# Attention and routed experts on one core: one VectorE copy for both banks of transposed probabilities, and batch 0's expert logits in four column groups

## What is computed

```python
x = x + tanh(g_xattn) * attention(layernorm(x), ctx, ctx, mask)   # qh, kh, vh: 16 heads of 64
x = x + tanh(g_ffn) * ffn(layernorm(x))

# ffn
logits = xf @ Wg + bg                       # [1024, 8]
idx = argmax(softmax(logits), axis=-1)
h = gelu(einsum('th,ehi->tei', xf, W1) + b1)
y = einsum('tei,eih->teh', h, W2) + b2
out = take_along_axis(y, idx)
```

## Time and profile before

| | |
|---|---|
| median of 3 runs | 199.1 us (198.98 to 364.73) |
| profiled execution | 200.14 us |
| its span, first to last instruction | 198.3 us |
| PE busy | 185.5 us, 94% |
| DVE, ACT, POOL busy | 123.5, 104.9, 89.5 us (62%, 53%, 45%) |
| attention loop of batch 0, of batch 1 | about 37 to 62 us, 110 to 137 us |
| between them | about 62 to 103 us |
| POOL's last start-up instruction (L594) | 3.70 us, 0.09 long |
| ACT's load of bg_sb (L784) and wg_sb (L785) | issued at 16.01 and 16.48 us |
| share of the chain of waits | PE 69%, DVE 21%, issue 3%, ACT 2% |

### The profile page before, as it was taken

The page is one execution under the profiler, slowest core; times in us unless marked ns, Lnnn a source line. Parts: engine busy times, 40 slices in busy tenths (PEclk is TensorE's granted clock), DMA queues, the critical chain, the costliest instruction groups (busy, mean ns, idle before and its releaser), DMA issues.

```text
span 198.3 us, 4265 instructions
## 1 busy us (share of the span) xinstructions
PE 185.5 (94%) x1412; PEld 136.2 (69%) x1412; DVE 123.5 (62%) x538; ACT 104.9 (53%) x376; POOL 89.5 (45%) x128
## 2 busy tenths in 40 slices
PE   7999999999899999999999899998999999999960
PEld 6994455666665444788895666765788899989940
DVE  3479576899996421154459999997833556355520
ACT  3243438899998112211427899997631263445410
POOL 6000002577778991000003899768810024776650
PEclk9999999999999999999999999999999999999996
DMA  4998008999999990480000101600000002353011
GB/s 134 335 369 284 0 3 265 319 287 315 298 317 266 206 326 20 146 279 1 0 2 3 55 27 54 198 0 0 3 0 2 0 3 76 110 153 109 34 53 31
DMA packets 22323, 25.19 MB, mean 127 GB/s; under 512 B 1987, under 2 KB 20877, under 8 KB 22160
## 3 DMA queue, kind: packets, MB, share of 16 engines
q1 hardware_dynamic: 19536, 21.83, 37.3%
q0 software_dynamic: 1152, 2.12, 3.2%
q10 hardware_dynamic: 1600, 0.84, 1.5%
HBM read 14.14 MB, written 11.68 MB: 130 GB/s over the span
## 4 chain that ended last, share of the span: by engine, by line
PE 69%; DVE 21%; issue 3%; ACT 2%; POOL 1%; POOLq 1%; DVEq 0%
PE s_bank L1729 14%; PE o_bank L1674 14%; DVE probs L1308 12%; PE s_bank L2035 8%; PE o_bank L2046 7%; PE s_bank L1769 5%; DVE oT L1335 4%; PE s_bank L1608 3%; PE s_bank L1639 2%; PE o_bank L1817 2%; PE o_bank L1799 2%; PE t_bank L1700 2%; PE s_bank L1844 2%; ACT probs L832 2%; PE s_bank L2024 1%
## 5 line engine op out<-in xcount | busy, mean ns | idle before, releaser
L649 POOL TENSOR_TENSOR probs<-probs,r_col 128x512 f32<-128x512 f32 x32 | 33.3, 1040 | 73.8 <-DVE r_col L1319 73.7
L832 ACT ACTIVATE probs<-probs,negm_run 128x160 f32<-128x160 f32 x128 | 53.0, 415 | 6.1 <-DVE negm_run L1308 5.9
L1308 DVE CUSTOM_DVE_ANT_0 probs<-s_bank,maskneg 128x160 f32<-128x160 f32 x128 | 33.3, 317 | 3.5 <-PE s_bank L1769 3.2
L1729 PE MATMUL s_bank<-xnT,wq_sb 128*128 128x512 f32 x64 | 29.0, 600 | 0.0
L1674 PE MATMUL o_bank<-wo_sb,oT 128*128 128x256 f32 x128 | 28.7, 380 | 0.0
L1674 PEld LDWEIGHTS o_bank<-wo_sb,oT 128*128 128x128 f32 x128 | 23.9, 190 | 3.5 <-issue 0.5
L832 ACT ACTIVATION_READ_ACCUMULATOR probs<-probs,negm_run 128x1 f32 x128 | 23.9, 187 | 0.0
L1769 PE MATMUL s_bank<-k_sb,q_sb 64*128 64x160 f32 x256 | 21.7, 306 | 0.0
L1729 PEld LDWEIGHTS s_bank<-xnT,wq_sb 128*128 128x128 f32 x64 | 11.7, 190 | 13.1 <-issue 12.8
L628 POOL DMA_INDIRECT out_dram<-oT x16 | 17.0, 1064 | 7.8 <-DVE oT L1256 5.9
L1769 PEld LDWEIGHTS s_bank<-k_sb,q_sb 64*128 64x128 f32 x256 | 18.0, 187 | 2.7 <-DVE negm_run L1308 1.5
(11 more groups left out here) (169 smaller groups left out, 299.6 us busy)
## 6 DMA issues: line engine op xcount, KB each, us to landing
sorted_rows<-empty_row SPq DMA_DIRECT2D x8, 1040.0 KB, 15.6
oT<-in_L_ffn_W_dram SPq DMA_DIRECT2D x1, 2048.0 KB, 18.2
q_sb<-in_L_ffn_W_dram SPq DMA_DIRECT2D x1, 2048.0 KB, 9.4
oT<-sorted_rows SPq DMA_DIRECT2D x1, 1040.0 KB, 5.2
oT<-sorted_rows SPq DMA_DIRECT2D x8, 130.0 KB, 2.3
wq_sb<-in_L_xattn_Wq_dram SPq DMA_DIRECT2D x2, 512.0 KB, 8.1
mask_sb<-in_mask_BxSxS_bk_dram SPq DMA_DIRECT2D x2, 512.0 KB, 8.9
wv_sb<-in_L_xattn_Wv_dram SPq DMA_DIRECT2D x1, 1024.0 KB, 10.8
```

The source lines that it names most:

```text
L649: nc.gpsimd.tensor_tensor(window_wide(u), window_wide(u), r.rearrange("p i h -> p (i h)") .unsqueeze(2).broadcast_to([P, 4, WIDE]), ALU.mu ...
L832: last = nc.scalar.activation(window_part(u, i, h), window_part(u, i, h), ACT.Exp, bias=negm_run[at], scale=-1.0, accum_out=l_run[at])
L1308: nc.vector.tensor_tensor_reduce(window_part(u, i, h), s_bank[u % 2][:, h, i * CK:i * CK + WK], maskneg[:, q, 0:WK], -SCALE, LARGEST, ALU. ...
L1729: last = nc.tensor.matmul(bank[m % 4], wq_sb[:, c, m * P:(m + 1) * P], xnT[:, c, b * N:(b + 1) * N], start=(c == 0), stop=(c == DC - 1))
```

## The change

In the attention loop DVE now copies both banks of `t_bank` in one instruction, and ACT copies the left part instead of a bank. In `values` the two waits change places: the left product (first on PE) waits for ACT, the wide one for DVE.

Batch 0's logits are no longer made tile by tile. `batch_logits` makes them transposed, with `wg_sb` (padded with zeros to 32 columns) as the stationary operand and the tokens moving: tile t's logits land on partitions 32t to 32t+31 of bank 5, a group of 32 columns of the array each. DVE copies the 128x128 block to SBUF (`take_logitT`), PE transposes it back (`batch_logits_back`), and `route_logits(0)` reads it from there. The block stands between the second and the third group of keys and the transpose back behind the third; the transposes of tile 3 move ahead of the second group. `wg_sb` and `bg_sb` are cleared first by two memsets on POOL, for which ACT waits before it starts their loads. Batch 1's logits stay as they were.

```diff
-        wg_sb = sb("wg_sb", [P, DC, E])
-        bg_sb = sb("bg_sb", [P, E])
+        wg_sb = sb("wg_sb", [P, DC, LEFT_E])
+        bg_sb = sb("bg_sb", [P, LEFT_E])
+        logitT = sb("logitT", [P, P])
...
-                sp.wait_ge(empty_ready, 2)
+                sp.wait_ge(empty_ready, 4)
...
+            nc.gpsimd.memset(wg_sb[:], 0.0).then_inc(empty_ready, 1)
+            nc.gpsimd.memset(bg_sb[:], 0.0).then_inc(empty_ready, 1)
...
+            act.wait_ge(empty_ready, 2)
...
-            def job_pT_wide(b, job):
-
-                act.wait_ge(first.ptrans_ready, 2 * (b * JOBS + job) + 1)
+            def job_pT_left(b, job):
+
+                act.wait_ge(first.ptrans_ready, 2 * (b * JOBS + job) + 2)
                 if job >= 1:
                     act.wait_ge(first.o_ready, b * JOBS + job)
-                nc.scalar.copy(wide_of_row_half[:, 1], bank[5].rearrange("p (u n) -> p u n", n=DH)).then_inc(first.pT_act, 1)
+                nc.scalar.copy(left_of_row_half, o_bank[:, :, HALF:HALF + P].rearrange("p r (i n) -> p r i n", i=2))\
+                    .then_inc(first.pT_act, 1)
...
+            def take_logitT():
+
+                dve.wait_ge(logit_ps, 1)
+                nc.vector.tensor_copy(logitT[:], bank[5][:, P:2 * P]).then_inc(logitT_taken, 1)
+
...
-            def job_pT_rest(b, job):
-
-                for part, (dst, src) in enumerate((
-                        (wide_of_row_half[:, 0], bank[4].rearrange("p (u n) -> p u n", n=DH)),
-                        (left_of_row_half, o_bank[:, :, HALF:HALF + P].rearrange("p r (i n) -> p r i n", i=2)))):
-                    dve.wait_ge(first.ptrans_ready, 2 * (b * JOBS + job) + 1 + part)
-                    if job >= 1:
-                        dve.wait_ge(first.o_ready, b * JOBS + job)
-                    nc.vector.tensor_copy(dst, src).then_inc(first.pT_dve, 1)
+            def job_pT_wide(b, job):
+
+                dve.wait_ge(first.ptrans_ready, 2 * (b * JOBS + job) + 1)
+                if job >= 1:
+                    dve.wait_ge(first.o_ready, b * JOBS + job)
+                nc.vector.tensor_copy(wide_of_row_half, t_bank[:].rearrange("p r (u n) -> p r u n", n=DH)).then_inc(first.pT_dve, 1)
...
+            def batch_logits():
+
+                pe.wait_ge(xt2_sb, QT)
+                by_tile = [bank[5][t * LEFT_E:(t + 1) * LEFT_E, P:2 * P] for t in range(QT)]
+                for t in range(QT):
+                    nc.tensor.matmul(by_tile[t], bg_sb[0:1, :], ones[0:1, :], start=True, stop=False)
+                for c in range(DC):
+                    for t in range(QT):
+                        last = nc.tensor.matmul(by_tile[t], wg_sb[:, c, :], xnT[:, c, t * P:(t + 1) * P], start=False,
+                                                stop=(c == DC - 1))
+                last.then_inc(logit_ps, 1)
+
+            def batch_logits_back():
+
+                pe.wait_ge(logitT_taken, 1)
+                nc.tensor.transpose(bank[5][:, 2 * P:3 * P], logitT[:], ident[:]).then_inc(logit_ps, 1)
...
                 def transposes(job):
                     if job >= 1:
 
-                        pe.wait_ge(first.pT_dve, b * PER + 2 * job)
+                        pe.wait_ge(first.pT_dve, b * JOBS + job)
...
                 def values(job):
                     quad = job // 2
-                    pe.wait_ge(first.pT_dve, b * PER + 2 * job + 2)
+                    pe.wait_ge(first.pT_act, b * JOBS + (job + 1))
...
-                    pe.wait_ge(first.pT_act, b * JOBS + (job + 1))
+                    pe.wait_ge(first.pT_dve, b * JOBS + (job + 1))
...
                 if where == "k1":
-                    tile_logits(2)
+                    xn2_transposes(3)
                 elif where == "k2":
-                    xn2_transposes(3)
+                    batch_logits()
                 elif where == "k3":
-                    tile_logits(3)
+                    batch_logits_back()
...
-                        tile_logits(0)
...
-                        tile_logits(1)
```

More of the change, by code:

```diff
@@ L314, in flamingo_kernel @@
         logit_ps = sem("logit_ps")
+        logitT_taken = sem("logitT_taken")
         count_ready = sem("count_ready")
@@ L858, in attend_window @@
                         fill(0)
-                    job_pT_wide(b, job)
+                    job_pT_left(b, job)
                 for k in range(1, 4):
@@ L1155, in route_logits @@
                 shape = [P, tiles, E]
-                logits = bank[5][:, at * E:(at + tiles) * E].rearrange("p (t e) -> p t e", e=E)
-                dve.wait_ge(logit_ps, r + 1)
+                if r == 0:
+                    logits = bank[5][:, 2 * P:3 * P].rearrange("p (t e) -> p t e", e=LEFT_E)[:, :, 0:E]
+                else:
+                    logits = bank[5][:, at * E:(at + tiles) * E].rearrange("p (t e) -> p t e", e=E)
+                dve.wait_ge(logit_ps, r + 2)
                 then(nc.vector.tensor_reduce(R.lmax[:], logits, AX.X, ALU.max))
@@ L1385, in attend_window @@
                         window_sum(b, 2 * job + 2)
-                    job_pT_rest(b, job)
+                    job_pT_wide(b, job)
                     also(job)
@@ L1400, in attend @@
                     nc.vector.tensor_copy(*k_dst(u + 1)).then_inc(S.k_dve, 1)
+                    also(f"k{u}")
                 dve.wait_ge(S.mask_ready, n + 1)
@@ L1442, in route_first_batch @@
             def route_first_batch(where):
-                if where == "k":
+                if where == "k1":
+                    take_logitT()
+                elif where == "k":
                     route_logits(0)
@@ L1696, in tile_logits @@
                         nc.tensor.matmul(bank[5][:, q * E:(q + tiles) * E].rearrange("p (t e) -> p t e", e=E),
-                                         ones[0:1, :], bg_sb[0:1, :].unsqueeze(1).broadcast_to([1, tiles, E]),
+                                         ones[0:1, :], bg_sb[0:1, 0:E].unsqueeze(1).broadcast_to([1, tiles, E]),
                                          start=True, stop=False)
                 for c in range(DC):
-                    last = nc.tensor.matmul(bank[5][:, at], xnT[:, c, tt * P:(tt + 1) * P], wg_sb[:, c, :], start=False,
+                    last = nc.tensor.matmul(bank[5][:, at], xnT[:, c, tt * P:(tt + 1) * P], wg_sb[:, c, 0:E], start=False,
                                             stop=(tt in LAST_ROUTED and c == DC - 1))
@@ L2006, in before_projection @@
                 pe.wait_ge(first.pT_act, (b + 1) * (PER if later_too else M))
-                pe.wait_ge(first.pT_dve, (b + 1) * PER)
+                pe.wait_ge(first.pT_dve, (b + 1) * (PER if later_too else M))
             for m in range(M):
```

5 lines of the change are left out of this document (3 added, 2 removed).

## The result

| | before | after |
|---|---|---|
| median | 199.04 us of 4 runs (198.57 to 364.73) | 200.74 us of 4 runs (199.98 to 200.81) |
| profiled execution, its span | 200.14, 198.3 us | 199.98, 198.2 us |
| PE busy | 185.5 us, 94% | 184.7 us, 93% |
| DVE, ACT, POOL busy | 123.5, 104.9, 89.5 us | 127.1, 101.5, 89.5 us |
| chain of waits: PE, DVE, ACT | 69%, 21%, 2% | 65%, 15%, 10% |

The ratio is 1.0085, with a 95% interval of 1.005 to 1.012: the change makes the kernel 1.7 us slower (the run of 364.73 us stands in the median of the table, but not in the ratio). That is clear of the scatter, and less than 2%.

The account below looks back on a forecast made before the run. The loop was taken as bound by the DVE-PE round trip, 3.87 us a job, not by ACT. Terms 0.66+0.05+0.85+0.44 = 2.00 took the median from 199.1 to 201.1 us, range 198.6 to 202.6.

Parts of the forecast that it names:

- the middle: PE work between the batches: logits passes removed 1.65, added 1.30, transpose back 0.20, wait 0.20; sum +0.05 us.
- batch 0's loop: Batch 0's attention loop: steps of 0.22 us at every second max, +0.66 by the output copy before the q projections.
- batch 1's loop: Batch 1's attention loop: later output copy plus DVE's longer leg where it normalises; max 6 comes 0.85 us late.
- batch 1's job 6: Last full chain of batch 1, through ACT's copy: 0.61 us to the wide values becomes 1.05, +0.44.
- The exchange of releasers: values() in the loop: left values wait for ACT behind eight exps, so the output copy is 0.22 us late.
- The two-bank copy: DVE's pT copy in the loop: holds DVE 1.10 us; free under PE's leg, +0.20 where DVE normalises.
- rival 3: Loop: the copy over two banks runs over its cover, up to 0.17 us a job, giving 203.1 us; chance 0.07.
- Rival 1: Loop: ACT is the bound, so 0.19 us is saved in each of twelve jobs, giving 196.9 us; chance 0.10.
- rival 2: Loop: the late start of the left values is absorbed, giving 199.0 to 199.6 us; chance 0.20.
- The block: Batch 0's logits on PE between the batches: 24 passes at 0.037 us plus a 0.41 drain, 1.30 added.
- The removal: Batch 0's old bias and logits tiles on PE: 1.65 us removed in all, 0.97 of it at most ahead.
- The signs: Traces to confirm the forecast: max gaps of 3.87 and about 4.08 us, idle ACT, batch 1's first max 0.7 later.

Follow-up runs that it names:

- e2: The kernel before with only the copies half: attention loop of after, old logits; body 155.60 us, ratio 1.0082 against before.
- e3: The changed kernel with ACT's left copy behind six of the eight exps instead of all; body 153.79 us, ratio 0.9983 against before.
- e5: The changed kernel with a second, unread 256-element ACT copy ahead of each left copy; body 156.60 us, ratio 1.015 against before.
- e7: The changed kernel with DVE copying only bank 4, bank 5 left out; body 154.31 us, ratio 1.0012 against before.
- e8: The changed kernel with POOL normalising only 2 of 32 left keys in batch 1 from unit 8; body 154.63 us, ratio 1.0023 against before.
- e9: The changed kernel with POOL normalising only 16 of 128 wide keys in batch 1 from unit 8; body 154.65 us, ratio 1.0035 against before.
- e1: The changed kernel with the attention loop of before, so only the logits half; body 152.83 us, ratio 0.9964 against before.
- e4: The kernel before with ACT copying 256 of its 512 elements, the rest left out; body 153.29 us, ratio 0.9978 against before.
- e6: e1 with the block of 24 logits passes made twice; body 153.75 us, ratio 1.016 against before.

## Why the prediction was right, and where its terms were off

The sum was 2.00 and the body grew by 1.64; the median went up 1.7. The sign, the mechanism and the place of the loss were right. That the total came so close is partly luck: the middle was put 0.64 too high and batch 1 0.27 too low, and the two errors offset each other in part. The terms against what the traces show:

| term | forecast | measured |
|---|---|---|
| batch 0's loop | +0.66 | +0.67 (the left small transposes behind it start at 61.38 before and 60.97 after, with a first max 1.08 earlier) |
| logits and the middle | +0.05 | -0.59 |
| batch 1's loop | +0.85 | +1.13 (19.54 from its first max to job 6's before, 20.67 after) |
| batch 1's job 6 | +0.44 | +0.43 (its wide values start 4.52 after its first max before, 4.95 after) |

**The exchange of releasers** was right in batch 0 to 0.01 in sum, and nearly so step by step: the left values start 4.32 after M (46.16 to 50.48) where 4.35 was worked out, the wide ones 0.63 later, the output copy 1.13 after these where PE is what it waits for (55.22 to 56.35). e2 shows the loss in this half alone, e3 that it goes with the copy's place, e5 that it is passed on one for one, six times. One detail differed: in job 4 of batch 0 DVE stood idle 0.15 between its first two maxes (the row at 50.51), and that job's exps and left values were 0.25 later than in the jobs before. The profile names no releaser for this idle time; it stands at the same place in after, e2, e3, e5, e7, e8 and e9 and in none of before, e1, e4 and e6, and what makes it stays open. The late step came one job sooner than forecast (4.06 in place of 3.87), and the output copy ahead of the q projections was 0.65 late all the same.

**The two-bank copy**: 1.10 worked out from two sizes, 1.11 measured (126.67 to 127.78), and e7 shows it free in batch 0. DVE doesn't set the pace in batch 0, and rival 3 is out. **Rival 1** (ACT as the bound) is out by e4, and **rival 2** (the late start is absorbed) by after's own gaps of 4.08 and 4.11.

**The middle** was mis-sized by 0.64, at three steps. The block, "24x0.037+0.41 = 1.30", took 0.92: the loads go at 0.15/8 and 0.38/16 us, 0.019 and 0.024 each, not at the 0.037 of L1830, and for 0.20 behind each of the two groups no weights are loaded, not for 0.41 once. That is 0.38. The removal, 0.97 ahead of the first keys, was 1.14: the stretch of the bias and tile 0's logits and transposes shrank from 1.15 (91.05 to 92.20) to 0.22, and the one from the last context transpose to the keys from 1.25 to 1.04. The rows of both, before:

```profile
92.20 3.46 PE o_bank L1674 x16
95.93 0.26 PE s_bank L1752
...
97.18 1.12 PE s_bank L1844 x8
```

and after, from the chain of waits:

```profile
90.63 0.22 PE t_bank L1700 x2
90.85 3.46 PE o_bank L1690 x16
94.59 0.26 PE s_bank L1785
95.06 0.43 ACT ctxT L829
95.63 1.32 PE s_bank L1877 x8
...
101.67 0.77 PE s_bank L1802 x8
```

Wait and transpose back were 0.17 and 0.14 instead of 0.20 each, 0.09 together; from the first keys to batch 1's scores it is 6.04 (95.63 to 101.67) where it was 5.49 with two tiles of logits in it, and -0.68+0.92+0.17+0.14 = +0.55. An estimate from the up to 4x of the Trainium skill (TensorEngine Tiling (Array Packing), Theoretical Speedup) had the block at 0.67 and the middle 0.6 shorter. The middle came out at that by luck, since the block didn't: it is 0.25 longer, the removal gave 0.17 more, and wait and transpose back took 0.09 less. The drain at a change of the mode that the Trainium skill states (TensorEngine Tiling (Array Packing), Key Properties) fits the twice 0.20, the only gaps in the block's loads and behind them; that a drain makes them isn't tested. The bounds of the term (0.75 to 2.7) held it. The choice of the value is what failed: of two near rows, half of what L1830 took a pass and the pace of L1830's loads, I took a pace that belongs to another moving size (256 columns, where the block has 128), and called it a floor.

**Batch 1** was short by 0.27 (1.29 against 1.56). The step was "L1241, 0.37": it was 0.52 in the two jobs that count, 0.30 together. The price of the norm was read at one place against POOL's work and used at another. e8 and e9 give it back, and 0.05 more in each of the two jobs (0.32 instead of 0.37).

**The signs** named at the end of the prediction: the gaps of 3.87 and 4.08, ACT idle before its exps (0.93 at the first of batch 1, where it was 0.71 in the earlier trace rows), the copy's 1.10 and the left values' 4.3 all came, but for the last gap of batch 0 (4.06, above). The memsets cost nothing, as forecast: they are over before 4 us, and the two loads are issued at 14.95 and 15.41. One was wrong as it was put: "the first max of batch 1 comes some 0.7 later than before". It came 1.00 earlier (111.96, in the earlier trace rows 112.96). 1.08 of that is the start of the execution. Measured from batch 0's first max it is 0.08 later, 0.67 from the loop less 0.59 from the middle:

```profile
112.57 0.43 ACT L838 ACTIVATE probs<-probs,negm_run 128x160 f32<-128x160 f32 x1 [0.93 <-DVE negm_run L1323]
```

A sign should be a distance between two instructions of the loop, never a time from the start.

## What to carry to other kernels

To hand a small copy to the less busy engine says nothing about when it will be done: ask what stands ahead of it in that engine's queue, and who waits for it first. Here one change of place, a copy of 0.35 us two exps sooner, was worth 1.25 us of body, with the same load on every engine. And where a period is held by the way from one engine to another and back, a delay enters at every return (here every second job), and e5 shows it one for one; count the returns, not the instructions.

## What the runs showed of the hardware

A tensor_scalar of 256 fp32 elements from SBUF to SBUF on VectorE lasted 0.40 us alone (e9), 0.60 beside a GpSimd tensor_tensor of 128 elements (after), and 0.77 where it started 0.63 ahead of the end of one of 512 elements (e7). Wherever it lasted longer than 0.40, it ended 0.14 to 0.16 behind the end of a GpSimd instruction. GpSimd's own instruction of 128 elements went from 0.40 to 0.45 where the tensor_scalar ended first. Copies of 1024 elements out of PSUM kept their length beside GpSimd's instruction of 1.04 (1.19 at 126.67 in after). A group of 16 fp32 passes with 128 rows and 32 columns of weights took 0.38 of loads, with 0.20 without a load ahead of it and 0.20 behind it. Over the eleven profiles the first stretch differs by 1.8 us, and the last, which no edit touched, by 1.0 (2.6 with e6). The memsets of the change lie in the first stretch, but the kernels with and without them overlap there (37.86 to 39.66 and 38.45 to 39.69). So an effect under 1 us is read from a distance inside the trace.
